# One decoder layer on one core: the bias behind the exp, four score buffers, and a new setup of the self attention

## The reference

```
scores = q @ k^T * 0.25 + bias[bucket(key - query), head]     # self attention, q, k, v from x @ w_qkv^T
attn   = softmax(scores);  out = (attn @ v) @ w_proj^T + b_proj
x1 = layernorm(x + out)
x2 = layernorm(x1 + softmax(x1 @ ctx^T / 16 by heads) @ ctx)    # cross attention, no bias
y  = per token one of 8 experts: layernorm, 256 -> 1024 -> 256 with relu, gated by a sigmoid
out = layernorm(x2 + y)
```

## Time and profile before

| | us |
|---|---|
| median of 3 runs | 1135.42 (1131.54 to 1135.56) |
| the profiled execution | 1131.16 |
| its span, first to last instruction | 1129.3 |
| mean granted TensorE clock | 0.915 of 2.4 GHz |
| busy: PE / DVE / ACT / POOL | 972.1 / 667.4 / 771.5 / 319.6 |

### The profile page before, as it was taken

The page is one execution under the profiler, slowest core; times in us unless marked ns, Lnnn a source line. Parts: engine busy times, 40 slices in busy tenths (PEclk is TensorE's granted clock), DMA queues, the critical chain, the costliest instruction groups (busy, mean ns, idle before and its releaser), DMA issues. The chain is left out here.

```text
span 1129.3 us, 17448 instructions
## 1 busy us (share of the span) xinstructions
PE 972.1 (86%) x5213; PEld 514.7 (46%) x5213; DVE 667.4 (59%) x1762; ACT 771.5 (68%) x1456; POOL 319.6 (28%) x311
## 2 busy tenths in 40 slices
PE   7089999998989899999999999996089888898891
PEld 2023333333433343333333333333089878898790
DVE  4056766666767677734444555465357766686672
ACT  2067767676767677889888987892068777767770
POOL 2021030211111111100220221021314666666664
PEclk8589998989899998999999998996589998898995
DMA  7968877768685957679668965740143433343351
GB/s 226 166 244 134 191 179 173 181 160 203 134 228 108 243 105 176 114 148 258 114 119 127 166 123 88 129 94 20 51 165 112 164 102 111 118 152 120 108 178 41
DMA packets 93728, 162.92 MB, mean 144 GB/s; under 512 B 18447, under 2 KB 41806, under 8 KB 89742
## 3 DMA queue, kind: packets, MB, share of 16 engines
q1 hardware_dynamic: 88592, 152.78, 57.7%
q0 software_dynamic: 5056, 9.20, 2.9%
HBM read 116.41 MB, written 49.54 MB: 147 GB/s over the span
## 5 line engine op out<-in xcount | busy, mean ns | idle before, releaser
L693 ACT ACTIVATE probs<-sc 128x512 f32<-128x512 f32 x1024 | 528.9, 608 | 136.7 <-DVE sc L778 102.0
L474 PE MATMUL sc<-qst,kst 57*128 57x512 f32 (+1 forms) x1024 | 272.0, 482 | 37.9 <-ACT probs L693 21.8
L778 DVE TENSOR_TENSOR sc<-sc,strip 128x308 f32<-128x308 f32 (+1 forms) x512 | 193.6, 430 | 98.5 <-PE sc L474 96.6
L474 PEld LDWEIGHTS sc<-qst,kst 57*128 57x128 f32 (+1 forms) x1024 | 120.8, 190 | 230.2 <-ACT probs L693 181.8
L486 PE MATMUL ot<-probs,vals 128*32 128x512 f32 x1600 | 224.2, 634 | 0.0
L1694 POOL DMA_INDIRECT f_rows<-s_x,f_get_ids x45 | 106.4, 2365 | 36.1 <-issue 24.3
L507 PE MATMUL ms<-xT,w_qkv 128*128 128x512 f32 x128 | 68.7, 666 | 22.3 <-DMA xT<-in_xT 19.4
L1552 ACT ACTIVATE f_h<-f_h_ps,f_par 128x384 f32<-128x384 f32 x104 | 64.3, 619 | 25.5 <-PE f_h_ps L1471 25.4
L1632 DVE TENSOR_TENSOR f_h_lo<-f_h,f_h_hi 128x384 fp32r<-128x384 f32 x104 | 56.9, 547 | 27.3 <-ACT f_h_hi L1553 26.9
L1170 POOL TENSOR_SCALAR veps<-mv_self 128x4 f32<-128x4 f32 x8 | 1.9, 232 | 229.3 <-DVE mv_self L836 229.3
L1553 ACT ACTIVATE f_h_hi<-f_h_ps,f_par 128x384 fp32r<-128x384 f32 x104 | 64.7, 622 | 0.0
(11 more groups left out here) (155 smaller groups left out, 1578.9 us busy)
## 6 DMA issues: line engine op xcount, KB each, us to landing
s_qk<-split SPq DMA_DIRECT2D x32, 512.0 KB, 4.8
strip<-in_w_all SPq DMA_DIRECT2D x16, 1024.0 KB, 12.6
f_raw<-in_w_all SPq DMA_DIRECT2D x14, 1024.0 KB
kst<-s_qk SPq DMA_DIRECT2D x96, 128.0 KB, 4.3
qst<-s_qk SPq DMA_DIRECT2D x96, 128.0 KB, 6.9
kst<-s_ctx_parts SPq DMA_DIRECT2D x96, 128.0 KB, 6.6
qst<-s_x_parts SPq DMA_DIRECT2D x96, 128.0 KB, 8.4
s_x_parts<-split SPq DMA_DIRECT2D x16, 512.0 KB, 8.8
```

What stands on the lines that cost most here:

```text
L474: nc.tensor.matmul(sc[j][:], kst[at:at + rows, i, P * c:P * c + P], qst[at:at + rows, i, :], start=True, stop=True).then_inc(scored, 1)
L693: nc.scalar.activation(probs[:, k % KEPT, j, :], sc[j][:], ACT.Exp, scale=scale).then_inc(exped, 1)
L778: nc.vector.tensor_tensor(sc[j][:, lo:hi], sc[j][:, lo:hi], band_backwards(rank_of(4 * g + j), at, hi - lo), ALU.add).then_inc(biased, 1)
```

## The change

1. **Bias as a factor.** In the first pass the strip holds exp(bias); the exp waits only for the scores, and VectorE multiplies the band in `probs`, in place, behind the exp. `weigh` waits for `biased` instead of `exped`. ScalarE makes the exponential of the row (`rel_row`), and `test_table` checks once that the factors lie between exp(-8) and exp(8). The exact program still adds.
2. **Four buffers.** `parts` has four buffers, in memory that belongs to the experts' `w_hi0`, each with a semaphore of its own.
3. **Rows of the operands.** The channels of q and k are permuted, so that the four slots of a channel are next to each other; `load_pair` has 8 DMAs per half of the heads instead of 12, with pieces of 8 KB, to 32 and to 16 partitions. High and low rows now alternate. The outputs' and inputs' channels are permuted to match; the residual of the cross attention is read with a step of 4 elements.
4. **Setup.** GpSimd fills the far rows from two constants per head into tiles that VectorE has cleared; the far matmul and its two roundings go. `w_qkv` comes in two DMAs, three inputs are issued by ScalarE, the second half of the strip and the late inputs later, `earlier` is only waited for in sequence 1.

```diff
-        parts, xparts = [four[:, 0], four[:, 1]], [four[:, 2], four[:, 3]]
+        spare = w_hi0.rearrange("p m (i s n) -> p (m i) s n", s=2, n=N)
+        parts, xparts = [spare[:, i] for i in range(4)], [four[:, 2], four[:, 3]]
...
             def load_pair(n, pair):
                 wait(sp, scored, UNITS * (n - 1) + 32 * (pair + 1))
                 if n < B:
-                    for s in st_parts:
-                        wait(sp, s, 16 * (2 * n + pair + 1))
+                    for s in st_parts[2 * pair:2 * pair + 2]:
+                        sp.wait_ge(s, 16 * (n + 1))
...
-                for src, dst, order in ((k_from, kst, (0, 1, 0)), (q_from, qst, (0, 0, 1))):
-                    for r, part in enumerate(order):
-                        two = src[part, P * pair:P * pair + P].rearrange("(i s d) n -> s d i n", s=2, d=D)
-                        for half in range(2):
-                            row = HALF * half + D * r
-                            sp.dma_start(dst[row:row + D, some, :].bitcast(F32), two[half]).then_inc(ld_pair[pair], 16)
+                for half in range(2):
+                    for src, dst in ((k_from, kst), (q_from, qst)):
+                        row, at = HALF * half, P * pair + HALF * half
+                        each = src[:, at:at + HALF].rearrange("t (d s) n -> d t (s n)", d=D)
+                        two = each if dst is kst else bass.AP(each.tensor, each[:, 0].offset, [each.ap[0], [0, 2], each.ap[2]])
+                        sp.dma_start(dst[row:row + 2 * D, some, :].bitcast(F32), two).then_inc(ld_pair[pair], 16)
+                        sp.dma_start(dst[row + 2 * D:row + 3 * D, some, :].bitcast(F32), each[:, 0 if dst is kst else 1]).then_inc(ld_pair[pair], 16)
...
-                pe.wait_ge(exped, UNITS * n + 4 * k + 4)
+                pe.wait_ge(biased if n < B and not exact else exped, UNITS * n + 4 * k + 4)
...
-                ready, scale = (biased, SELF_SCALE) if n < B else (scored, CROSS_SCALE)
+                ready, scale = biased if n < B and exact else scored, SELF_SCALE if n < B else CROSS_SCALE
...
             def high_qk(b, i):
                 act.wait_ge(qk_mm, 4 * b + i + 1)
-                wait(act, st_parts[i % 2], 16 * (2 * b + i // 2))
-                nc.scalar.activation(parts[i % 2][:, 0, :], ms[i % 2][:], ACT.Copy).then_inc(qk_hi, 1)
+                wait(act, st_parts[i], 16 * b)
+                nc.scalar.activation(parts[i][:, 0, :], ms[i % 2][:], ACT.Copy).then_inc(qk_hi, 1)
...
                 for j in heads:
-                    dve.wait_ge(scored, UNITS * b + 4 * k + j + 1)
-                    nc.vector.tensor_tensor(sc[j][:, lo:hi], sc[j][:, lo:hi], band_backwards(rank_of(4 * g + j), at, hi - lo),
-                                            ALU.add).then_inc(biased, 1)
+                    dve.wait_ge(scored if exact else exped, UNITS * b + 4 * k + j + 1)
+                    some = sc[j][:, lo:hi] if exact else probs[:, k % KEPT, j, lo:hi]
+                    nc.vector.tensor_tensor(some, some, band_backwards(rank_of(4 * g + j), at, hi - lo),
+                                            ALU.add if exact else ALU.mult).then_inc(biased, 1)
...
+            def fill_far():
+                pool.wait_ge(ld_far_in, 16)
+                nc.gpsimd.tensor_scalar(far_scaled, far_tab, 1.0 / SELF_SCALE, None, ALU.mult).then_inc(far_zero, 1)
...
+                for part, value, filled in ((far_hi_part, far_tab_hi, far_hi), (far_lo_part, far_tab_lo, far_lo)):
+                    for c in range(NC):
...
+                                last = nc.gpsimd.tensor_copy(part[:, c, some].bitcast(F32R),
+                                                             value[:, side:side + 1].to_broadcast([H, some.stop - some.start]))
```

More of the change, by code:

```diff
@@ L2 @@
 import concourse.bass as bass
+import math
 import numpy as np
@@ L427, in load_first @@
-                some = SLOTS // 2
-                for part in range(2):
-                    for half in range(2):
-                        at = SLOTS * half + some * part
-                        sp.dma_start(strip[:, at:at + some, :],
-                                     bass.AP(scratch["rel"].tensor, SPAN * at, [[1, P], [SPAN, some], [1, BAND]])).then_inc(ld_strip[part], 16)
+                far = scratch["far"]
+                sp.wait_ge(far_hi, 2)
+                sp.dma_start(far[:, 0].rearrange("c h n -> h c n"), far_hi_part).then_inc(st_far, 16)
@@ L655, in tensor_program @@
             pe.wait_ge(ld_w, 16)
-            for i in range(2):
+            for i in range(4):
                 project_qk(0, i)
-            pe.wait_ge(ld_far_in, 48)
-            for c in range(NC):
-                last = nc.tensor.matmul(sc[c][0:H, :], far_tab, far_mask[:, c, :], start=True, stop=True)
-            last.then_inc(far_mm, 1)
-            for i in range(2, 4):
-                project_qk(0, i)
+            pe.wait_ge(ld_wv, 16)
             for i in range(2):
@@ L747, in cross_body @@
                         sigmoid_exp(c - 1)
-            for i in range(2):
-                high_qk(0, i)
-            act.wait_ge(far_mm, 1)
-            for c in range(NC):
-                last = nc.scalar.activation(far_hi_part[:, c, :].bitcast(F32R), sc[c][0:H, :], ACT.Copy, scale=1.0 / SELF_SCALE)
-            last.then_inc(far_hi, 1)
-            for i in range(2, 4):
+            nc.scalar.dma_start(far_tab, io["far_table"]).then_inc(ld_far_in, 16)
+            nc.scalar.dma_start(krows, io["krows"]).then_inc(ld_rows, 16)
+            nc.scalar.dma_start(qrows, io["qrows"]).then_inc(ld_rows, 16)
+            if not exact:
+                act.wait_ge(rel_mm, 1)
+                nc.scalar.activation(rel_row, ot[0:H, 0:SPAN], ACT.Exp).then_inc(rel_sb, 1)
+            for i in range(4):
                 high_qk(0, i)
@@ L1054, in self_body @@
                     add_band(b, k, (0, 1))
+                    if b == 1 and k == 0:
+                        dve.wait_ge(ld_earlier, 16)
+                        nc.vector.tensor_copy(earlier[:], earlier_f32)
                     if b > 0:
```

145 lines of the change are left out of this document (85 added, 60 removed).

## The result

The changed kernel takes **1090.46 us** (median of 4 runs, 1087.96 to 1093.02), the kernel before 1134.77 beside it: a ratio of 0.9615, 95% interval 0.9585 to 0.9645. The forecast was 1051, its range 1024 to 1084: the sign was right, and the gain about half of the forecast one. The rest of this text looks for the missing 40 us.

What follows compares the result with a forecast made beforehand. It saw exps waiting for the bias, projections for stores, and TensorE as the steady-sequence floor. Setup -24.2, sequence 0 -4.5, steady sequences -39.6, sequence 7 -6.9, loads -5 gave -80.2: from 1131.16 to 1051 us, range 1024 to 1084.

Steps and rivals of the forecast that it cites:

- Term 1: Steady self-attention sequence: TensorE's own work, with 0.8 us for longer exps, sets a floor of 45.4 us at full clock.
- Term 2: Steady sequences: VectorE loses 4.3 us to GpSimd, 2.1 unhidden; 47.5 us each, -39.6 for six.
- the two-block slack: `weigh` comes two blocks after its block's multiplications, about 3 us, hiding VectorE's lateness except at `norm_x` and `low_qk`.
- Rival C: Steady sequences: waits for x1 or xT keep the clock at 0.94, some 3 us more each; 1069 us, chance 0.09.
- Sequence 7: Last self-attention sequence, no projections ahead: 37.3 plus 0.7 for the lock, 38 us, -6.9.
- Term 3: Setup: far-row delay and wait for `earlier` go, pair load shortens; first exp at 31.5 us, -24.2; sequence 0 another -4.5.
- I take 12: Setup: pair load taking 12 us from first issue to landing, where pair and far rows took 16.5.
- Sequence 0: First self-attention sequence: from 49.5 to 45 us, -4.5, with TensorE still waiting for xT in block 0.
- Term 4: Cross-attention loads: fewer DMA issues on SP bring pass 5's pair load 1.9 us earlier; -5 taken for that pass.
- Rival B: VectorE becomes the bound: 51 us a steady sequence, sequence 7 at 42; 1076 us, chance 0.14.

Runs made afterwards that it cites:

- the constants alone: Changed kernel with GpSimd's addition of x and output bias and its context split replaced by memsets to constants: 1087.9 us, ratio 0.9653.
- the early reading alone: Changed kernel with the sums bank read between the halves of a block's multiplications instead of behind them: 1089.77 us, ratio 0.968.
- both 15.7: Changed kernel with sums read between the multiplication halves and GpSimd's bias addition and context split writing constants: 1080.15 us, ratio 0.9554.
- the move of xT: Changed kernel with sums read between multiplication halves, GpSimd writing constants, and xT's load issued ahead of x1's store: 1074.0 us, ratio 0.9496.
- the addition: Changed kernel with the bias again added in PSUM ahead of the exp; buffers, loads and setup as changed: 1076.18 us, ratio 0.9531.
- the narrow loads: Changed kernel with pair loads as twelve transfers to 16 partitions, keeping the long pieces: 1100.7 us, ratio 0.9739.
- both moves: Changed kernel with sums read between multiplication halves and xT's load ahead of x1's store, nothing left out: 1082.59 us, ratio 0.9549.
- both versions with GpSimd moved: Changed kernel, sums read between multiplication halves, xT loaded before x1's store, GpSimd's bias addition earlier, context split from block 5 or 7: 1071.04 and 1068.18 us.

## Why the prediction missed

**Term 1, the floor of 45.4 on TensorE: right to 1 us.** With the disturbances taken away a sequence takes 46.4.

**Term 2, what VectorE's lateness costs: this is the step that failed.** The lock itself was right in kind. The term took half of GpSimd's time as lost and let "the two-block slack" hide all but 2.1 us. Measured from the floor of 46.4, the changed kernel loses 4.3 us, so that 47.5 became 50.7. Over the six sequences these are 25.5 us (304.2 against 278.7): the constants alone gave back 11.0 (three half-clock spells fewer among it), or 1.8 a sequence, which is about the 2.1 of the forecast; the early reading alone 4.1; both 15.7; and the move of xT 9.8 more. Three things failed. First, the slack ("about 3 us of slack, so nothing at first") was counted for `weigh` waiting for the multiplications, but VectorE's queue also holds readings that have no such slack: the reading of the sums bank, which `weigh` of the next group waits for at once (blocks 2, 10 and 14). The prediction named `norm_x` and `low_qk` as moving back and left `turn_sums` out. Its own last sentence, that `weigh` waiting for the multiplications would prove it wrong in kind, came true in sequence 0 only. Second, it asked how much of GpSimd's time VectorE pays, while the total hardly matters: 39.6 us of held multiplications with sequences of 46.9 us, 31.7 with those of 50.7. Third, it put the wait for xT near zero: with lock and queue both gone TensorE waits 1.2 to 2.2 us for it in five of the six sequences, which then take 48.1 in the mean, still more than the 47.5 of the forecast.

**The gain of the factor.** That the factor frees the exps is true (9.3 us of waits behind additions against 4.4 behind scores), but the sequence of the addition is 48.8, only 2.4 above the floor of 46.4. So in this order of the queues the factor had 2.4 us to gain and lost 4.3: the addition was better. The prediction credited buffers and factor together and so never asked what the addition alone would give.

**Rival C** (waits that pull the clock down) was there as a companion: with the wait of 1.64 us at block 14 comes a half-clock spell in five of the six steady sequences, at 1.4 us a spell. That the wait is the cause is not shown: with two buffers the same wait stood there six times, and two spells came. The wait was one for `weigh`, not for x1 or xT as that rival had it.

**Sequence 7** was forecast from TensorE and ScalarE (37.3) plus 0.7 for the lock. It took 46.1, with GpSimd's constants 41.7, with these and the early reading 40.2. So 4.4 us are the lock and 1.5 the reading, and the 37.3 was 2.9 too low even without both. This rest was not tried apart, but the trace of the last of these runs places most of it: blocks 14 and 15 took 8.2 us, against 5.8 in its steady sequences, with a wait of 1.58 us for the sums bank, whose reading stands behind `norm_x`, and a half-clock spell.

**Term 3.** The wait for `earlier` and the far rows went as forecast. The step "I take 12" for the pair load failed: 16.4, as long as before. The three reasons given for it (far loads ahead, half of the strip away, longer pieces) bought nothing here; in other executions it took 12.1 to 16.5, and why is open. Sequence 0, -4.5 forecast and +1.2 measured, is the lock again (45.6 with constants).

**Term 4:** -5 forecast in the cross attention, -4.6 measured. Pass 5 went from 40.8 to 35.7, and pass 2 gave back 1.7. The number is partly luck: the kernel before with four buffers still has the twelve transfers, and its pass 5 took 37.0 and its cross attention 4.6 less as well. That SyncE's fewer issues gave the gain is not shown.

**The range.** Rival B's 51 us a sequence was nearly the truth, but by luck: it had VectorE as the bound, which was busy for 41.9 of 50.8 us, and as busy in sequences of 46.9. Its 1076 joined the 51 us to a sequence 7 of 42 and to an undisturbed setup; all three terms missed to the same side, since two of them hang on the same lock.

## What to carry to other kernels

When an operation is moved behind another engine's work, go through everything that is queued behind it on its own engine, and ask of each how soon somebody waits for it: the slack of the operation itself says nothing of the slack of what follows. A lock between two engines is priced by the place where it falls, not by its length: before cutting work, try moving it to blocks where nothing is due. Of a change with several parts, ask what each gives on top of the others; here the part that sounded best took back about a fifth of what the rest had gained (0.9531 to 0.9615).

## What the runs showed of the hardware

- A multiplication of two SBUF tiles that takes 0.42 us lasts until shortly after GpSimd is done when GpSimd reads SBUF beside it: 1.0 to 1.3 us beside a cast of 1.0 to 1.3, and 1.4 to 2.7 beside an operation of 2.4 to 2.5. When GpSimd only writes (memsets of 0.95 us) it takes no more than 0.48. The Trainium skill, "SBUF — State Buffer", section "SBUF: two separate sides", tells of a lock for the whole instruction, against GpSimd operations that read; the changed kernel and the runs with constants agree.
- When two operations of GpSimd follow each other, VectorE gets one multiplication done for each: in sequence 0 two operations of 2.44 and 2.50 us held one of 2.56 and one of 2.52, and each ended 0.24 us after its operation.
- TensorE's wait of 1.63 us at block 14 came with a spell at half the clock in five of six steady sequences of the changed kernel and in five of six with the narrow loads, but in two of six with two buffers, though it was as long in all of them. With a wait of 1.28 us there (early reading, constants, both moves) it was nine of eighteen, and with 0.85 us (both versions with GpSimd moved) one of twelve.
- The first pair load, 1.5 MB in pieces of 8 KB to 48 partitions of each half, took 12.2 us with nothing issued behind it, and 12.1 to 16.5 with 2.8 MB issued behind it; two kernels with the same setup differed by as much as 2.6 us.
